# Routing of the first batch moved ahead of its gated activations, five early banks, and attention's output rearranged and divided through memory

## The reference

```
x = x + 0.5 * ffn(layernorm(x))     # h = silu(xn @ Wg[e]) * (xn @ Wu[e]);  out = sum_e w[t,e] * (h @ Wd[e])
x = x + attn(layernorm(x))          # ctx = softmax(causal(q k^T / 4)) v;   ctx @ Wo.T + bo
x = x + 0.5 * ffn(layernorm(x))
```

## Time and profile before

| | us |
|---|---|
| median of three runs | 779.62 |
| the three runs | 779.62, 780.57, 778.31 |
| the profiled execution, its time | 779.27 |
| the profiled execution, its span | 777.5 |
| PE busy | 758.5 (98%) |
| DVE, ACT, POOL busy | 476.2, 348.5, 417.0 (61%, 45%, 54%) |

### The profile page before, as it was taken

One profiled execution on the slowest core, in us unless ns is written; L12 is line 12 of the kernel. 1 busy time (PEld: TensorE's weight loads), 2 busy tenths in 40 slices (PEclk: granted clock), 3 DMA queues, 4 the chain that ended last, 5 costly groups with the idle time before them and its releaser, 6 DMA issues.

```text
span 777.5 us, 14076 instructions
## 1 busy us (share of the span) xinstructions
PE 758.5 (98%) x4878; PEld 606.8 (78%) x4878; DVE 476.2 (61%) x1316; ACT 348.5 (45%) x657; POOL 417.0 (54%) x497
## 2 busy tenths in 40 slices
PE   6979999999999999999999999999999999999998
PEld 5868878976778777777778778677777778888887
DVE  6847754596657857787556667855657433473333
ACT  4455425525446544656344456453463453423222
POOL 4384867246654444844454853454554655655663
PEclk9999999999999999999999999999999999999999
DMA  9236423363213631323531222433222132223231
GB/s 304 84 103 192 163 74 105 103 201 96 70 55 92 177 101 62 103 62 106 161 117 48 82 86 89 140 97 109 77 89 83 48 104 82 82 67 124 84 117 58
DMA packets 60807, 81.57 MB, mean 105 GB/s; under 512 B 8384, under 2 KB 44608, under 8 KB 60736
## 3 DMA queue, kind: packets, MB, share of 16 engines
q1 hardware_dynamic: 58544, 80.36, 32.5%
q10 hardware_dynamic: 2192, 0.32, 0.2%
HBM read 67.78 MB, written 12.71 MB: 104 GB/s over the span
## 4 chain that ended last, share of the span: by engine, by line
PE 90%; DVE 6%; POOL 1%; issue 1%; DMA 1%; ACT 0%; DVEq 0%; POOLq 0%
PE ra L746 15%; PE ra L747 14%; PE ra L748 14%; PE dn L768 8%; PE dn L769 7%; PE dn L770 7%; PE ra L879 5%; PE ra L867 5%; PE ra L852 5%; PE ra L723 3%; PE ra L820 1%; PE ra L834 1%; PE ra L835 1%; PE ra L836 1%; PE ra L797 1%
## 5 line engine op out<-in xcount | busy, mean ns | idle before, releaser
L1357 POOL TENSOR_TENSOR hid<-hid,wb 128x512 f32<-128x512 f32 x124 | 161.5, 1303 | 183.0 <-DVE hid L1218 176.8
L746 PE MATMUL ra<-xt_hi,wgu_hi 128*128 128x512 f32 x512 | 226.5, 442 | 0.0
L1361 POOL TENSOR_TENSOR ht_lo<-hid,ht_hi 128x512 fp32r<-128x512 f32 x124 | 162.0, 1308 | 120.2 <-ACT ht_hi L997 119.8
L747 PE MATMUL ra<-xt_hi,wgu_lo 128*128 128x512 f32 x512 | 203.1, 397 | 0.0
L748 PE MATMUL ra<-xt_lo,wgu_hi 128*128 128x512 f32 x512 | 202.4, 395 | 0.0
L1269 DVE CUSTOM_DVE_ANT_0 junk<-ra,mask 128x128 bf16<-128x128 f32 (+3 forms) x256 | 121.0, 487 | 84.0 <-PE ra L852 81.3
L768 PE MATMUL dn<-wd,ht_hi 128*128 128x256 f32 x512 | 162.6, 318 | 2.7 <-POOL ht_lo L1361 2.7
L1210 DVE SCALAR_TENSOR_TENSOR hid<-hid,ra 128x512 f32<-128x512 f32 x125 | 85.7, 686 | 125.0 <-ACT hid L989 124.0
L769 PE MATMUL dn<-wd,ht_hi 128*128 128x256 f32 x512 | 144.9, 283 | 0.0
L770 PE MATMUL dn<-wd,ht_lo 128*128 128x256 f32 x512 | 144.5, 282 | 0.0
L997 ACT ACTIVATE ht_hi<-hid 128x512 fp32r<-128x512 f32 x124 | 78.0, 630 | 144.0 <-POOL hid L1357 119.4
(11 more groups left out here) (164 smaller groups left out, 859.4 us busy)
## 6 DMA issues: line engine op xcount, KB each, us to landing
wd<-wd_parts SPq DMA_DIRECT2D x56, 512.0 KB, 3.6
wb<-wts_rows SPq DMA_DIRECT2D x62, 256.0 KB, 3.7
qk_parts<-parts SPq DMA_DIRECT2D x32, 192.0 KB, 2.1
q_st<-qk_parts SPq DMA_DIRECT2D x96, 64.0 KB, 2.2
k_st<-qk_parts SPq DMA_DIRECT2D x96, 64.0 KB, 2.2
wd_parts<-wd SPq DMA_DIRECT2D x8, 512.0 KB, 3.0
x_res<-in_x SPq DMA_DIRECT2D x4, 512.0 KB, 8.5
stage<-in_Wg SPq DMA_DIRECT2D x8, 256.0 KB, 5.3
```

What stands on the lines that cost most here:

```text
L746: mm(b_, w_hi, xt_hi[q % 2][:, c, :], start=c == 0, stop=False)
L747: mm(b_, w_lo, xt_hi[q % 2][:, c, :], start=False, stop=False)
L1357: nc.gpsimd.tensor_tensor(tb, tb, wb[m % NWB][:, :], ALU.mult).then_inc(hw_done, 1)
L1361: nc.gpsimd.tensor_tensor(ht_lo[n % NHT][:, :], hidden(n)[:, :], f32(ht_hi[n % NHT][:, :]), ALU.subtract).then_inc(lo_done, 1)
```

## The change

The first FFN block's routing is due at once (all 8 pieces from -1.5), and the broadcasts of its weights at 1.60 in place of 2.90. The first 5 chunks may hold 5 of the 6 ring banks for gates and ups in place of 3. Early down projections are due at 3.6 + 0.87 n in place of 4.6 + 0.75 n. Block 1's preparation, with the statistics of batches 1 to 3 and their Newton steps, starts 2 chunks later (Q1 = 7.0 in place of 5.0), after the routing.

In attention, `t1` and `t2` (all transposes of the context) are gone. Per group, SP stores `cx` to memory (`cs`), loads the context rows of the 4 heads back as 64 partitions of `cn`, features on the partitions, and one copy of the denominators as 128x16 (`cl`, two transfers); DVE takes the reciprocal of that; SP stores it (`rs`) and loads it back with every head's row repeated on 16 partitions (`rl`). Per half p of the features DVE multiplies `cn` by these rows (`nm`, 128x512), ACT makes `ct_hi` and DVE `ct_lo`, now from `cn` in SBUF and not from a bank. `wo` is due 0.7 chunks later and needs both halves. `junk` shrinks from 4 to 2 tiles.

```diff
-NBANK, NA, NG = 6, 4, 3
-NHID, NHT = 3, 2
+NBANK, NA, NG, NG_FIRST = 6, 4, 3, 5
+NHID, NHT, NJUNK = 3, 2, 2
...
+FIRST_CHUNKS = 5
+Q1 = 7.0
+DOWN0, DOWN1 = 3.6, 0.87
...
-        down[n] = n + LAG + 0.66 if n >= EARLY else 4.6 + 0.75 * n
+        down[n] = n + LAG + 0.66 if n >= EARLY else DOWN0 + DOWN1 * n
...
-    put(2.90, ("wbp", 0))
-    put(2.92, ("wbp", 1))
-    put(2.95, ("wt", 0))
+    put(1.60, ("wbp", 0))
+    put(1.62, ("wbp", 1))
+    put(1.65, ("wt", 0))
...
-        put(3.6 + 0.2 * j, ("stats", 1, j))
-    put(4.9, ("var", 1))
-    put(5.1, ("newton", 1, 0))
-    put(5.4, ("newton", 1, 1))
+        put(Q1 - 1.6 + 0.2 * j, ("stats", 1, j))
+    put(Q1 - 0.1, ("var", 1))
+    put(Q1 + 0.1, ("newton", 1, 0))
+    put(Q1 + 0.4, ("newton", 1, 1))
     for k in range(ROUTE_PIECES):
-        put(0.02 + 0.25 * k, ("route", 0, k))
+        put(-1.5 + 0.1 * k, ("route", 0, k))
...
-        start = CB * (q - 1) + {4: 2.2, 6: 6.8, 7: 8.2}.get(q, 5.0)
+        start = CB * (q - 1) + {1: Q1, 4: 2.2, 6: 6.8, 7: 8.2}.get(q, 5.0)
...
-            put(meet[g + 1] + 1.3, ("t1", b, g))
+            put(meet[g + 1] + 1.0, ("cs", b, g))
+            put(meet[g + 1] + 1.4, ("cl", b, g))
+            put(meet[g + 1] + 1.8, ("rec", b, g))
+            put(meet[g + 1] + 2.0, ("rs", b, g))
+            put(meet[g + 1] + 2.4, ("rl", b, g))
         for p in range(2):
-            put(meet[GR] + 2.4 + 0.2 * p, ("t2", b, p))
-            put(meet[GR] + 3.0 + 0.5 * p, ("wo", b, p))
+            put(meet[2 * p + 2] + 2.6, ("nm", b, p))
+            put(meet[GR] + 2.8 + 0.2 * p, ("ct", b, p))
+            put(meet[GR] + 3.7 + 0.5 * p, ("wo", b, p))
...
-                if in_use[side] >= (NG if side == "g" else NA):
+                first = side == "g" and o["takes"][1] < FIRST_CHUNKS
+                if in_use[side] >= (NG_FIRST if first else NG if side == "g" else NA):
...
+                then=[("dve", "route", 0, ROUTE_PIECES - 1)] if it == ("stats", 1, 0) else [])
...
-            add("pe", ("t1", b, g), 0.45, ("act", "pv", b, g), ("pe", "t2", b - 1, 1) if g == 0 and b else None)
-            add("dve", ("t1", b, g), 0.7, ("pe", "t1", b, g))
+            add("sp", ("cs", b, g), 0.4, ("act", "pv", b, g), kb=256)
+            add("sp", ("cl", b, g), 0.9, ("sp", "cs", b, g), ("dve", "ct", b - 1, g // 2) if b and g % 2 == 0 else None,
+                ("dve", "rec") + ago(1) if G else None, kb=136)
+            add("dve", ("rec", b, g), 0.26, ("sp", "cl", b, g), ("sp", "rl") + ago(1) if G else None)
+            add("sp", ("rs", b, g), 0.4, ("dve", "rec", b, g), kb=8)
+            add("sp", ("rl", b, g), 0.4, ("sp", "rs", b, g), held, kb=128)
...
-            add("pe", ("t2", b, m), 0.45, ("dve", "t1", b, GR - 1))
-            add("act", ("t2", b, m), 0.5, ("pe", "t2", b, m), ("pe", "v", b + 1, 1) if b + 1 < BATCH else None)
-            add("dve", ("t2", b, m), 0.6, ("act", "t2", b, m))
-            add("pe", ("wo", b, m), 1.42, ("dve", "t2", b, m))
+            add("dve", ("nm", b, m), 0.69, ("sp", "rl", b, 2 * m), ("sp", "rl", b, 2 * m + 1), ("sp", "cl", b, 2 * m + 1), port=True)
+            add("act", ("ct", b, m), 0.53, ("dve", "nm", b, m), ("pe", "v", b + 1, 1) if b + 1 < BATCH else ("pe", "wo", b - 1, 1))
+            add("dve", ("ct", b, m), 0.69, ("act", "ct", b, m), port=True)
+            add("pe", ("wo", b, m), 1.42, ("dve", "ct", b, 0), ("dve", "ct", b, 1))
...
+                    if kind == "cs":
+                        sp.wait_ge(*emptied(("pv", b, g)))
+                        sp.dma_start(cx_dram[b, g], cx[:, :]).then_inc(cx_st, 16)
+                    if kind == "cl":
+                        parts_of = cx_dram[b, g].rearrange("(h w f) t -> w h f t", w=2, f=HD)
+                        sp.wait_ge(cx_st, 16 * (G + 1))
+                        sp.dma_start(cn[rows, p, :], parts_of[0]).then_inc(cn_ld, 16)
+                        sp.dma_start(den[:, :], parts_of[1, :, 0, :]).then_inc(den_ld, 16)
+                    if kind == "rs":
+                        sp.wait_ge(rec_done, b * GR + g + 1)
+                        sp.dma_start(rec_dram[b, g].rearrange("h t -> (h t)").rearrange("(p c) -> p c", p=P),
+                                     rec[:, :]).then_inc(rec_st, 16)
+                    if kind == "rl":
+                        sp.wait_ge(rec_st, 16 * (G + 1))
+                        sp.dma_start(rec_rows[rows, :], rec_dram[b, g].unsqueeze(1).to_broadcast([GH, HD, T])
+                                     ).then_inc(row_ld, 16)
```

More of the change, by code:

```diff
@@ L416, in plan @@
                 needs = [("dve", "add", b)]
-            add("dve", it, 0.8, *needs, ("dve",) + pieces[j - 1] if j else None)
+            add("dve", it, 0.8, *needs, ("dve",) + pieces[j - 1] if j else None,
+                then=[("dve", "route", 0, ROUTE_PIECES - 1)] if it == ("stats", 1, 0) else [])
         add("dve", ("var", k), 0.4 + 0.3 * len(batches), ("dve",) + pieces[-1])
@@ L435, in plan @@
         for k in range(ROUTE_PIECES):
-            needs = [("act", "route", q, 0)] if k == 0 else [("dve", "route", q, k - 1)]
+            needs = [("act", "route", q, 0)] if k == 0 else []
             if k == 0 and q:
@@ L442, in plan @@
                 needs.append(("pe", "wt", q - 1))
-            add("dve", ("route", q, k), length[k], *needs, port=True)
+            add("dve", ("route", q, k), length[k], *needs, port=True, then=[("dve", "route", q, k - 1)] if k else [])
         add("act", ("route", q, 1), 0.35, ("dve", "route", q, 0))
@@ L591, in build @@
         vf = sb("vf", [P, QT, H, 2 * HD])
-        junk = sb("junk", [P, NA, T], BF16)
+        junk = sb("junk", [P, NJUNK, T], BF16)
         mx = [sb(f"mx{i}", [P, GH * QT]) for i in range(2)]
@@ L607, in over @@
             return nc.alloc_sbuf_tensor_at(name, shape, dt, offset=at)
-        ct_hi = [over(f"ct_hi{i}", [P, KT, HT], F32R, x2_at + 2048 * i) for i in range(2)]
-        ct_lo = [over(f"ct_lo{i}", [P, KT, HT], F32R, x2_at + 4096 + 2048 * i) for i in range(2)]
+        ct_hi = over("ct_hi", [P, KT, T], F32R, x2_at)
+        ct_lo = over("ct_lo", [P, KT, T], F32R, x2_at + 4096)
         stage = [over(f"stage{i}", [P, KT, 3 * D], F32, probs_at + 6144 * i) for i in range(NSTAGE)]
@@ L1051, in _ @@
                         if b + g > 0:
-                            act.wait_ge(ra_full, full(("t1", b, g - 1) if g else ("t1", b - 1, GR - 1)))
+                            act.wait_ge(cx_st, 16 * (b * GR + g))
                         nc.scalar.activation(cx[:, :], o[:, :], ACT.Copy).then_inc(freed, 1)
-                    if kind == "t2":
+                    if kind == "ct":
                         b, p = it[1:]
-                        if p == 0 and b + 1 < BATCH:
-                            act.wait_ge(ra_full, full(("v", b + 1, 1)))
-                        nc.scalar.activation(ct_hi[p][:, :, :], o[:, :].rearrange("p (c t) -> p c t", c=KT),
-                                             ACT.Copy).then_inc(chi_done, 1)
+                        act.wait_ge(ra_full, full(("v", b + 1, 1) if b + 1 < BATCH else ("wo", b - 1, 1)))
+                        act.wait_ge(nm_done, 2 * b + p + 1)
+                        nc.scalar.activation(ct_hi[:, p, :], cn[:, p, :], ACT.Copy).then_inc(chi_done, 1)
             @block.vector
```

94 lines of the change are left out of this document (53 added, 41 removed).

## The result

| | before | changed |
|---|---|---|
| median, us | 779.71 | 771.44 |
| runs, lowest to highest | 5, 778.31 to 780.57 | 5, 771.13 to 772.32 |
| ratio, with 95% interval | | 0.9898 (0.9886 to 0.9910) |
| profiled execution: time, span | 779.27, 777.5 | 771.44, 769.7 |

The change saves 1.0%, 8 us. The forecast was 764.2, a saving of 15.1 us; the sign was right, the size was not, and half of it is missing. 771.44 lies at the upper edge of the range given (760 to 771.5), where the case "the front gives nothing" stood (770.9).

What follows compares the result with a forecast made beforehand. PE's own work was taken to bound the kernel. From 779.3 us, 6.7 (early stretch) and 9.7 (transposes) came off, 0.5 (DVE holds) and 0.8 (late `wo`) were added: 764.2 us, range 760 to 771.5.

Steps and rivals of the forecast that it cites:

- the front gives nothing: Rival, chance 0.09: early routing in one run piles up DVE's work, another wait replaces POOL's; 770.9 us.
- What bounds the kernel: Whole kernel: PE's own work sets the pace, busy 462.97 of 464.00 us from 193 to 657 us.
- The early hole, 6.7 us: PE at 42 to 54 us: waits for POOL's low parts and a lowered clock cost 6.7 us, all saved.
- Block 1 ... cost nothing, the cover is six chunks: Block 1's preparation, 2 chunks later: transposes needed at chunk 16, due at 9.3 and 9.7, so no cost.
- The transposes, 9.7 us: Attention, 193 to 657 us: removing 96 transposes from PE saves 9.7 us, bounds 8.4 and 10.6.
- A price by the rows' durations, 26 us: Rival, chance 0.02: the 96 transposes cost what their trace rows say, 26.2 in place of 9.7 us; 748 us.
- 0.5 for holds: DVE in attention: multiplication and low part with both operands in SBUF are held; 0.5 us on the path, bounds 0 and 18.
- 0.8 for a late `wo`: Last attention batch: memory trips make `wo` and block 7's preparation 2 to 3 us later; cost 0.8 us, bounds 0 and 3.
- The new work on DVE: DVE in attention: reciprocals, multiplications and low parts replace similar ones; no new load, nothing charged beyond holds.
- The trips through memory (rival, 0.08): Attention, chance 0.08: trips estimated 2 to 3 us too short make PE wait for `wo` at 4 places; 776 us.
- SP's queue (rival on the other side, 0.07): Chance 0.07: trips in SP's queue delay broadcasts 2.1 us beyond cover in 16 groups, losing 34 us; 798 us.

Runs made afterwards that it cites:

- mended front alone: The kernel before with only the early-stretch edits, but timed routing links for blocks 1 to 7 and Q1 = 5.0; attention through transposes: 774.13 us.
- Attention's part: The changed kernel with every early-stretch edit undone (due times, banks, links as before), attention through memory: 769.44 us, ratio 0.9864.
- mended kernel: The changed kernel with routing links of blocks 1 to 7 timed in the plan again and Q1 = 5.0 in place of 7.0: 765.96 us, ratio 0.9814.

## Why the prediction was right and wrong

- **What bounds the kernel.** Right: PE, full from 193 to 657 us in both, with losses only where routing and attention's head meet.
- **The early hole, 6.7 us.** Right as far as it went. Chunk 12 is 6.8 us earlier, and the mended front alone saves 5.9 us. The steps in it were rough, though. The routing of block 0 ends at 22.35 + 0.22 us, not at 21.2. Its later instructions keep the pace that was worked out, but the first one took 1.42 us beside a POOL pass (held as those above), instead of 0.2: it ends at 17.41 us with POOL's `wgu_lo`. The broadcasts stand at 25.23 us in PE's order, not at 22.44: one chunk more goes before them. POOL's first pass is at 27.07, against 24.1 as forecast and 32.01 before:

```profile
27.07 1.29 POOL L1370 TENSOR_TENSOR hid_a<-hid_a,wb 128x512 f32<-128x512 f32 x1 [9.70 <-ACT wb L995]
```

 That is 4.9 us sooner, where 7.9 were forecast, and it was enough: no wait for `ht_lo` is left and the clock is whole from 40 to 54 us. That PE would stop with three banks was right (1.66 us), though the total of the changed kernel is the same with them.
- **"Block 1 ... cost nothing, the cover is six chunks".** This is the step that failed. The cover was read from due times, but PE's order isn't built from due times alone: the turn `wt` stands where the plan believes the weights ready. Block 1's preparation moved 2 chunks back, and its `wt` moved with it (56 of the matmuls counted above stand ahead of it where 50 did, 1.5 chunks). So there was no cover of six chunks, only what lies between the plan's time for the routing and the chip's. With it the edit of the links was passed over, which stands in the diff and applies to all blocks: it costs 3.0 us net on the kernel before, where it packs block 0's routing too, and 3.1 us come back in the changed one when blocks 1 to 7 get their times again. Links and start together are 14.5 - 8.0 = 6.5 us, of the 15.1 - 8.0 = 7.1 that are missing. This term was 0 in the sum, and measures 6.5. PE loses most of them waiting for `wts` of blocks 1 and 2, 2.12 and 2.72 us, with the clock at its lower level behind the second.
- **The transposes, 9.7 us.** Right. Attention's part saves 10.6 us net of its costs (9.0 to 12.2), and from chunk 28 to the end 9.1 us. A price by the rows' durations, 26 us, is out. The net forecast was 8.4, a little too low; the 0.5 for holds and 0.8 for a late `wo` can't be seen as costs, and the one wait that grew with this part alone, for block 5's weights by 1.2 us, was not among the terms.
- **The new work on DVE.** Right in kind. The groups of the changed kernel that answer to the earlier trace rows:

```profile
L1300 DVE TENSOR_TENSOR ct_lo<-cn,ct_hi 128x512 fp32r<-128x512 f32 x8 | 6.6, 822 | 3.8 <-ACT ct_hi L1070 3.8
L1296 DVE TENSOR_TENSOR cn<-cn,rec_rows 128x512 f32<-128x512 f32 x8 | 5.9, 735 | 2.1 <-DMA rec_rows<-rec_rows_of 2.1
```

 The low part from SBUF takes 822 ns in the mean against 690 from a bank, at worst 1371: 8 x 0.13 = 1.1 us of hold, plus 8 x 0.05 at the multiplication. That is 1.5 us where 2.4 was reckoned, none of it seen on the path. That an instruction with a single input in SBUF is not held, as the prediction had it, is too wide: in this trace `tensor_scalar` is (1.14 us, in the last section). Nothing in the sum rested on that half.
- **The trips through memory (rival, 0.08).** They are longer than worked out. For the last batch, ACT's and SP's timelines:

```profile
639.51 0.60 ACT L1065 ACTIVATE cx<-ra 128x512 f32<-128x512 f32 x1 [2.04 <-PE ra L904]
```

```profile
640.13 0.32 SPq L1455 DMA_DIRECT2D ctx_rows<-cx  x1
642.18 0.54 SPq L1463 DMA_DIRECT2D cn<-ctx_rows  x1
642.76 0.52 SPq L1466 DMA_DIRECT2D den<-ctx_rows  x1
646.10 0.32 SPq L1421 DMA_DIRECT2D wd<-wd_parts  x1
646.83 0.33 SPq L1432 DMA_DIRECT2D wb<-wts_rows  x1
647.20 0.42 SPq L1470 DMA_DIRECT2D rec_rows_of<-rec  x1
650.41 0.54 SPq L1478 DMA_DIRECT2D rec_rows<-rec_rows_of  x1
```

 The first `wo` matmul starts at 658.4, 18.9 us behind `cx`, where 13.5 was the estimate and 11.9 the old distance. The store of 8 KB needs 3.2 us to land (650.41 - 647.20), twice the 1.6 of the row taken for it. The load of the denominators, issued at 642.76, is there only as DVE starts the reciprocal at 646.32, 3.6 us later where 2.2 were taken. Yet PE waits nowhere for `ct_lo` in the changed kernel: `wo` stands later in its order, with FFN matmuls ahead of it. The last routing waits 1.41 us where it waited 1.26.
- **SP's queue (rival on the other side, 0.07).** Didn't come. In the waits of POOL that reach a us or more none is for a reloaded `wb` but the first (9.7 us, down from 14.6).
- **The front gives nothing (rival, 0.09).** Nearly right in its number, 770.9, and for another reason than given. The waits came neither from a bank nor from a staged weight, but from the routings of the blocks behind. Its price is right by luck: 6.5 us lost there, where it took 6.7.

With that term the sum closes: 764.2 + 6.5 = 770.7 against 771.44. The mended kernel, 765.96, is within 1.8 us of the sum without it.

Left open is whether GpSimd's low part can be kept off the routings without leaving it out; a version that does was not tried.

## What to carry to other kernels

A step that is moved in a static order brings along its consumers: don't read the cover of a move from its due times, but count in the trace what stands between the end of the step and the in-order engine's use of it, and compare with how long the step takes in the trace. Read every line of a diff for its scope; a dependence that loses its time in a planner is an edit to every block, here worth 3 us net alone and 6.5 together with a moved start. And split a change at the first result: two runs showed that one half gave all and the other nothing.

## What the runs showed of the hardware

A GpSimd pass that reads SBUF holds even DVE's smallest instructions until it ends. In the changed kernel 25 routing instructions of 4 to 32 elements per partition took 0.48 to 1.42 us in place of about 0.2, and 24 of them end within 0.1 us of the end of a GpSimd pass. Among them are some with one input, as this one beside a pass of POOL that ends at 345.41 us (344.13 + 1.28):

```profile
344.30 1.14 DVE L1111 TENSOR_SCALAR sums<-sums 128x4 f32<-128x4 f32 x1
```

The same page of the Trainium skill has a place for that too: it lists `tensor_scalar` among the operations that can take both of DVE's port pairs. In the run with writes in place of the subtraction such an instruction is held to the end of a write as well (0.56 us beside a pass of 0.53), while 28 instructions with two inputs are not. The hold is as long for 4 elements per partition as for 32 (1.26 and 1.29 us at worst in blocks 1 and 2), so it weighs most in a chain of tiny instructions: four holds put 4 us onto the 12.8 of block 1's routing.
